# Attention loop of a decoder layer: prefills moved behind a read back, a clearing copy moved ahead of an eviction, a bias product moved one step later

## The reference

```python
def attn(x, Wv, bv, Wo, bo):                  # 16 heads of 8, 64 tokens, 64 batches
    p = einsum('bsd,ed->bse', x, Wv) + bv     # q = k = v = p, by heads
    attn = softmax(einsum('bhqd,bhkd->bhqk', p, p) / sqrt(dk))
    out = einsum('bhqk,bhkd->bhqd', attn, p)
    return einsum('bsd,ed->bse', out, Wo) + bo
x = x + attn(layernorm(x), ...)
x = x + xattn(layernorm(x), ctx, ctx)         # same softmax, keys = values = ctx, no weights
h = layernorm(x)                              # router, 7 experts, shared expert
x = x + 0.5 / w * swiglu(h, shared) + p / w * swiglu(h, expert of the token)
```

## Time and profile before

| | us |
|---|---|
| runs | 422.83, 423.81, 423.74 |
| median | 423.74 |
| profiled execution, its own time | 422.83 |
| its span | 420.6 |
| TensorE busy | 397.2 (94%) |
| VectorE, ScalarE, GpSimd busy | 300.7, 298.3, 282.7 |

### The profile page before, as it was taken

How to read it: one execution, slowest core, us unless ns; L and a number is a source line. 1 busy time by engine, 2 the same in 40 slices (tenths; PEclk the granted TensorE clock), 3 DMA queues, 4 the chain that set the end, 5 groups by cost and what they waited for, 6 DMA issues and landing times.

```text
span 420.6 us, 16171 instructions
## 1 busy us (share of the span) xinstructions
PE 397.2 (94%) x5545; PEld 309.8 (74%) x5546; DVE 300.7 (71%) x790; ACT 298.3 (71%) x683; POOL 282.7 (67%) x471
## 2 busy tenths in 40 slices
PE   8879999999989899989999989799999999999996
PEld 5555666666656566656666656699999999999995
DVE  5538989999989899988999778774344444444444
ACT  7867989998989899889999847432223566666641
POOL 8557878888878888887888526247777464444441
PEclk9989999999999999999999999999999999999999
DMA  6144364545464555445343499602223355520001
GB/s 106 40 67 69 56 87 73 88 68 85 66 83 75 64 93 72 70 76 63 56 53 52 36 192 250 187 27 83 84 89 103 93 139 145 139 82 26 29 32 52
DMA packets 180195, 35.21 MB, mean 84 GB/s; under 512 B 145491, under 2 KB 177622, under 8 KB 180128
## 3 DMA queue, kind: packets, MB, share of 16 engines
q1 hardware_dynamic: 170096, 24.54, 35.9%
q0 software_dynamic: 2816, 6.10, 4.2%
q10 hardware_dynamic: 7216, 3.69, 3.2%
HBM read 20.86 MB, written 15.67 MB: 87 GB/s over the span
## 4 chain that ended last, share of the span: by engine, by line
PE 63%; SPq 13%; DMA 8%; DVE 7%; issue 6%; ACT 2%; POOL 0%; DVEq 0%; POOLq 0%; ACTq 0%
PE psum L816 20%; SPq L195 13%; PE psum L875 10%; PE psum L614 8%; PE psum L623 8%; DMA orow<-attention_out 6%; PE psum L635 5%; PE psum L645 2%; PE psum L602 2%; DVE pr_s L1224 2%; PE psum L718 1%; PE psum L713 1%; PE psum L757 1%; PE psum L911 1%; DVE mx_x L1209 1%
## 5 line engine op out<-in xcount | busy, mean ns | idle before, releaser
L1399 DVE TENSOR_TENSOR gT<-gT,psum 128x384 f32<-128x384 f32 x66 | 36.6, 554 | 69.5 <-ACT gT L1112 41.7
L1112 ACT ACTIVATE gT<-psum 128x384 f32<-128x384 f32 x70 | 34.0, 486 | 46.8 <-PE psum L816 39.0
L462 POOL TENSOR_TENSOR k_s<-pT,hmask_sb 128x1024 f32<-128x1024 f32 x32 | 60.9, 1903 | 6.2 <-ACT pT L1018 6.2
L575 POOL DMA_INDIRECT out<-yrow,token x38 | 37.0, 973 | 40.1 <-DVE yrow L1532 35.4
L875 PE MATMUL psum<-wdn_sb,gT 128*128 (+1 forms) x420 | 58.3, 275 | 0.0
L816 PE MATMUL psum<-fhT,wtile 128*128 128x128 f32 x456 | 57.1, 275 | 0.0
L816 PEld LDWEIGHTS psum<-fhT,wtile 128*128 128x128 f32 x456 | 53.9, 192 | 0.0
L1209 DVE TENSOR_REDUCE mx_s<-psum 128x16 f32<-128x1024 f32 x32 | 39.2, 1225 | 20.2 <-PE psum L614 20.2
L875 PEld LDWEIGHTS psum<-wdn_sb,gT 128*128 128x128 f32 x420 | 52.5, 192 | 0.6 <-issue 0.4
L816 PE MATMUL psum<-hT_all,wup_sb 128*128 128x128 f32 x384 | 48.4, 276 | 1.4 <-ACT gT L1112 1.4
L816 PEld LDWEIGHTS psum<-hT_all,wup_sb 128*128 128x128 f32 x384 | 45.4, 192 | 1.6 <-ACT gT L1112 1.6
(11 more groups left out here) (183 smaller groups left out, 867.2 us busy)
## 6 DMA issues: line engine op xcount, KB each, us to landing
ring<-sorted_rows SPq DMA_DIRECT2D x30, 130.0 KB
sorted_rows<-nowhere_row SPq DMA_DIRECT2D x38, 65.0 KB, 3.0
wup_sb<-in_wup SPq DMA_DIRECT2D x7, 352.0 KB, 8.8
ring<-in_ctxv SPq DMA_DIRECT2D x64, 32.0 KB, 3.5
attention_out<-on_s SPq DMA_DIRECT2D x62, 32.0 KB
orow<-attention_out SPq DMA_DIRECT2D x31, 64.0 KB, 2.6
sorted_rows<-nowhere_row SPq DMA_DIRECT2D x3, 650.0 KB, 9.7
cross_keys<-in_ctxk ACTq DMA_DIRECT2D x14, 128.0 KB, 3.6
```

Source lines behind the costliest of these rows:

```text
L462: nc.gpsimd.tensor_tensor(k_s[:], pT[:].rearrange("p (b k) -> p b k", b=NB).unsqueeze(2).broadcast_to([P, NB, HG, S]), hmask_sb[:, 0:HG].u ...
L575: pool.indirect_dma_start(out=out, out_offset=bass.IndirectOffsetOnAxis(ap=token[p][:, 0:1], axis=0), in_=yrow[p][:, :], in_offset=None, b ...
```

## The change

Four moves; no instruction is added or removed.

- SyncE: the prefills and the `wo_turn` loads go behind the read back and the keys; the `wo_turn` loads are in steps 16 to 23, not 6 to 13.
- TensorE: the bias product is at the end of step 2, not of step 1.
- TensorE: the fillers are 1, 4, 4 in steps 1, 2, 3, not in steps 0, 1, 2.
- ScalarE: the ones and the clearing copy go ahead of the second exponential of the cross softmax, and so of the eviction of `oT_s`.

```diff
@@ SyncE, body @@
-                for tile in prefill_of_step(t):
-                    load(sp, hs_tiles[:, tile, 0:HALF], nowhere_row[:, 0:HALF], "prefilled")
-                if 6 <= t < 6 + P // H:
-                    load(sp, wo_turn[H * (t - 6):H * (t - 5), :, :], wo.rearrange("(q d) e -> q d e", d=DK), "l_turn")
                 if live("out") and u["out"] < U - 1:
                     sp.wait_ge(sem("s_out"), 16 * NB * at(u["out"]))
...
+                for tile in prefill_of_step(t):
+                    load(sp, hs_tiles[:, tile, 0:HALF], nowhere_row[:, 0:HALF], "prefilled")
+                if 16 <= t < 16 + P // H:
+                    load(sp, wo_turn[H * (t - 16):H * (t - 15), :, :], wo.rearrange("(q d) e -> q d e", d=DK), "l_turn")
@@ TensorE, body @@
-                if t == 1:
+                if t == 2:
                     pe.wait_ge(sem("l_second"), N_SECOND)
                     pe.wait_ge(sem("prepared"), 2)
                     nc.tensor.matmul(ps_bias, bvrows_sb[:], wo_sb[:], start=True, stop=True).then_inc(sem("bias"), 1)
-                if t < 3:
-                    keep_clock(1 if t == 0 else 4, bank[3])
+                if t in (1, 2, 3):
+                    keep_clock(1 if t == 1 else 4, bank[3])
@@ ScalarE, body @@
                     exp("x", u["pv_x"], 0)
+                if t == 1:
+                    act.wait_ge(sem("vx_zero"), 1)
+                    for h2 in range(2):
+                        ones = sums_of(vx[:, :, :].rearrange("p u c -> p (u c)"), h2)
+                        nc.scalar.activation(ones, zero[S * h2:S * (h2 + 1), 0:1].unsqueeze(2).broadcast_to(list(ones.shape)),
+                                             ACT.Exp).then_inc(sem("vx_ready"), 1)
+                if t == 2:
+                    nc.scalar.copy(kx_second, zero[:, 0:1].broadcast_to([P, CHUNK * NB * HG * S])).then_inc(sem("kx_zero1"), 1)
                 if live("pv_x"):
                     exp("x", u["pv_x"], 1)
...
```

More of the change, by code:

```diff
@@ L1054, in body @@
                     query(u["q"])
[L1055 to L1062, removed]
             phase_a(body, last=LAST_FULL)
```

## The result

| | before | changed | ratio, 95% interval |
|---|---|---|---|
| median us | 423.38 (5 runs) | 427.60 (5 runs, 426.48 to 428.47) | 1.0103 [1.0067, 1.0139] |
| profiled execution, span | 420.6 | 425.3 | |

The change makes the kernel slower, by 4.2 us. The forecast was 421.5, faster, and the range ended at 424.9.

A forecast was written before the change was run, and what follows sets the result against it. The prediction took TensorE to bound the attention loop, with waits for the read back into `orow` on top. Loop -4.8 and start +2.9 gave -1.9 us: 420.9 profiled, median 421.5, range 419.3 to 424.9.

The forecast's parts named there:

- What bounds the loop, and the size of the wait: Attention loop, steps 5 to 30: TensorE bounds; removing its wait for the read back into `orow` gains at most 5.4 us.
- Part 1: SyncE's order, steps 6 to 31: read back leaves at 3.4, not 4.5 us; gain 4.8 us, between 1.5 and 5.4.
- SyncE's step: Doubled steps of the loop: SyncE needs 6.7 to 7.3 us, taken as 6.8, against the loop's 7.00.
- rival 3: Steps 16 to 23: SyncE becomes the bound, deciding from about 7.1 us per step; +1.8, about 425.2 us; chance 0.08.
- The landing: Read back in the loop, issue to landing: 3.2 us as in step 33, 1.8 at best; within the 7.28 budget.
- rival 4: Loop: without a prefill ahead the read back lands slower, disturbed steps still wait; +1.4, about 424.8 us; chance 0.09.
- Part 2: Start, steps 1 to 3: maxima of unit 1 4.8 us later, 1.1 back from the clock; loss 2.9, bounds 2.0 and 5.7.
- The sum: Whole kernel: -4.8 in the loop and +2.9 at the start make -1.9 us; new median 421.5.
- rival 1: Start eats the loop's gain: loss 4.8 to 5.7 against 4.8, 0 to +0.9, about 423.8 us median; chance 0.22.

The follow-up runs named there:

- np_start: no_prefill_in_loop with all three start edits of the change (clearing copy, bias product, fillers): 440.15 us, 0.9947 to the kernel before.
- np_again: The same kernel as no_prefill_in_loop, run once more as base on the chip of np_start: 436.14 us, 0.9870 to the kernel before.
- np_fill: no_prefill_in_loop with four fillers added in step 3 (1, 4, 4, 4 in steps 0 to 3): 431.99 us, 0.9823 to the kernel before.
- no_prefill_in_loop: The kernel before with the 38 prefills taken out of the loop and issued after it in four loads: 417.77 us, 0.9863 to before.
- np_fill_wo: np_fill with the `wo_turn` loads behind the keys in steps 16 to 23, as in the change: 432.66 us, 0.9846 to the kernel before.
- bias_only: The kernel before with only the bias product moved to the end of step 2: 424.60 us, 1.0014 to before.
- fill_only: The kernel before with only the fillers moved (1, 4, 4 in steps 1 to 3): 423.22 us, 0.9979 to before.
- start_only: The kernel before with TensorE's and ScalarE's moves alone, SyncE's order as before: 428.32 us, 1.0103 to before.
- copy_only: The kernel before with only ScalarE's clearing copy and the ones moved ahead of the eviction of `oT_s`: 427.03 us, 1.0044 to before.

## Why the prediction was wrong

- **What bounds the loop, and the size of the wait**: right. 5.4 us at most by the earlier trace rows; taking the prefills out gained 5.1 in the loop between the profiled executions. How much there is to gain differs between executions, though: six with the old order took 177.6 to 184.4 us there, against 175.0 without waits.
- **Part 1, when the read back leaves**: wrong, and here the gain was lost. The step said "the read back then leaves at about 3.4 in place of 4.5". I had read 3.4 from step 33, the one kind of step whose preceding step has no prefill either. With prefills right ahead of the stores on the queue the stores landed 4.2 us after their issue on average in steps 14 to 26, so the read back left at 4.18. The prediction had no term for this. A load that is moved behind one transfer is moved ahead of the next one; I asked only who was behind it in its old place.
- **SyncE's step, "I take 6.8"**: wrong by the same 0.8 us. The other terms held (keys 1.4, prefills 0.8 to 1.35, `wo_turn` 0.43); in steps 16 to 23 SyncE's step was 7.57 us on average, 7.2 to 8.1. That is over the threshold of 7.1 of rival 3, which I had given 0.08, and SyncE was all but never idle before the stores, the sign set for it. Its reason was another: not the prefills stalled behind the keys, the stores landed late behind the prefills. Its sum, 1.1 us still gained in the loop, was too good too; the profiled execution had 0.4 lost. The sum of the durations of an issuing engine over one step has to be made with its waits in it, and the wait for the stores was the largest of them.
- **The landing**: 3.2 was too pessimistic for the changed kernel, where the median from issue to landing was 2.3 us (1.7 to 3.6). In the kernels without prefills, whose read back leaves soonest, it was 2.7 to 2.9: a part of an earlier issue is taken back by the landing, as rival 4 had it, but not most of it. The estimate from the Trainium skill, "DMA: Bandwidth & Descriptors", section "Anatomy of one DMA — SWDGE (gpsimd) path", 2.15 us, is near the median of the changed kernel's trace, 2.3, and 0.6 to 0.8 under that of the kernels without prefills. The waits did not go in the changed kernel.
- **Part 2, the chain of the start**: the mechanism was right in each link, the size too small. Loss 2.9 was forecast, within 2.0 and 5.7; it was 4.5 in the profiled execution and 4.0 by medians of np_start against np_again. The mis-sized term is the delay of the maxima, +6.6 in place of +4.8. The 1.8 went with two stretches at the lower clock; the one in the gap of step 2 I had bounded at 0.9, the one near 8 us I had not considered, as I had put the filler of step 0 down as giving nothing. The landing was short, 3.53 in place of 4.65, and that was no luck of one execution: it was 4.63 to 4.70 in all ten with the start of before (np_fill and its two relatives counted), and 2.4 to 3.6 in all eight with another start. The 6.25 us to the second L713 came as forecast, but it is not the change's gain: with the start of before and no filler in step 3 three of seven executions had 6.25 too, and the 7.30 that I read as the price of a clock fall was one of the other four. Against those three, step 5 of the changed kernel came 5.5 us later, not 4.5.
- **The sum**: +4.5 and +0.4 in the loop, less 0.2 at the end, is the 4.7 us between the spans. A start of 4.5 with the loop's 4.8 gained would have been rival 1's "no change"; what made the change slower is that the loop gave nothing.

## What to carry to other kernels

A transfer moved out of the way on a queue comes to stand in front of something else; look at who comes next on the queue, and whether that one is on the same path a step later. Before giving an issuing engine more work behind a wait, add up its step with the waits in it and compare it with the loop's step. Where bulk work can leave a latency-bound loop altogether, that can beat any place inside it: here it gained 1.4%, the two other places tried in the loop nothing, and the four runs of each such kernel lay within 0.7 to 2.3 us. At a start, two small delays on one engine's queue are not additive when one stands behind the other.

## What the hardware showed that I had not expected

- Prefills of 65 KB ahead of two stores of 32 KB moved the stores' landing from 3.4 or 3.5 us to 4.0 to 4.2 on average in steps 14 to 26, where SyncE itself spent only 0.4 us on issuing one. In steps 6 to 13 they landed late without prefills too (4.30 us in no_prefill_in_loop, 3.74 in np_fill_wo), so something else delays them there.
- Kernels whose loop has the same instructions in the same order differ widely there in single executions: 177.59 us for steps 5 to 30 in bias_only (42.22 to 219.81) and 184.39 in fill_only (41.14 to 225.53), with the clock at its lower level for 3.4 us in the latter. Without prefills seven executions lay between 175.35 and 175.70. Most of the spread is in the waits on `orow`.
- TensorE's clock fell after only 0.95 us without work near 8 us, in the changed kernel and in start_only, but not in np_start and fill_only with the same program order and a gap of 0.96 us there.
- The read back of step 3 took 4.63 to 4.70 us to land in ten executions with the same start, and 2.81 in fill_only, which issued it at the same time. In the ten a packet of 16 KB of an instruction queue starts 2.5 us after the issue and runs for 1.0 us; in fill_only it starts at 26.64 us, after the landing at 26.15. The one shorter landing, 2.38 us in copy_only, has it behind the landing too. That the packet is the cause is not shown by an experiment.
